# In each step of an attention kernel, TensorE issues the piece of the maxima ahead of the high products instead of between the high and the low products

## The reference

```python
# layer 0, attention over the 4096 positions of a batch, on gn(x)
f = Wq @ xf + bq;  g = Wk @ xf + bk      # 32 channels each
h = Wv @ xf + bv                          # 256 channels
s = einsum('bki,bkj->bij', f, g)          # 4096 x 4096
beta = softmax(s, axis=1)                 # over i
x = x + gamma * einsum('bci,bij->bcj', h, beta)
# layer 1, on gn(x)
y = bn_relu(w1 @ x + b1)                  # 32 channels
packed = all 528 products y[r] * y[c]
x = x + bn_relu(w2 @ packed + b2)
```

## Time and profile before

| | |
|---|---|
| median of three runs | 2136.95 us (2135.04 to 2138.11) |
| the profiled execution's own time | 2135.18 us |
| its span, first to last instruction | 2133.4 us |
| TensorE, matmuls busy | 2081.3 us, 98% |
| DVE busy | 1623.2 us, 76% |
| ScalarE busy | 1608.0 us, 75% |
| GpSimd (POOL) busy | 1321.3 us, 62% |
| mean granted TensorE clock | 0.999 of full |

### The profile page before, as it was taken

How to read it: one execution, slowest core, us unless ns; L and a number is a source line. 1 busy time by engine, 2 the same in 40 slices (tenths; PEclk the granted TensorE clock), 3 DMA queues, 4 the chain that set the end, 5 groups by cost and what they waited for, 6 DMA issues and landing times.

```text
span 2133.4 us, 48577 instructions
## 1 busy us (share of the span) xinstructions
PE 2081.3 (98%) x17838; PEld 1640.4 (77%) x17838; DVE 1623.2 (76%) x3491; ACT 1608.0 (75%) x2582; POOL 1321.3 (62%) x1984
## 2 busy tenths in 40 slices
PE   4899999999999999999999999999999999999999
PEld 2688888888878877877878777777887778777854
DVE  7687877778877777877778887776876767777767
ACT  4577877777777777878777787777877777777767
POOL 3254455556566676776657677676756656566656
PEclk9999999999999999999999999999999999999999
DMA  6054555455467776667378576776635555464622
GB/s 204 21 81 75 75 88 83 84 84 82 81 119 141 138 135 143 135 118 139 71 149 152 117 142 119 142 143 126 130 59 114 117 103 113 97 122 76 118 66 80
DMA packets 592493, 233.63 MB, mean 110 GB/s; under 512 B 541024, under 2 KB 547936, under 8 KB 592224
## 3 DMA queue, kind: packets, MB, share of 16 engines
q1 hardware_dynamic: 592256, 230.53, 56.4%
HBM read 71.83 MB, written 19.92 MB: 43 GB/s over the span
## 4 chain that ended last, share of the span: by engine, by line
PE 92%; DVE 2%; ACT 2%; issue 1%; DMA 1%; SPq 1%; POOL 0%; DVEq 0%; ACTq 0%
PE acc L1763 21%; PE acc L1751 20%; PE acc L1752 20%; PE sps L1576 5%; PE tps L1556 5%; PE acc L1556 5%; PE tps L1627 4%; PE acc L1550 3%; PE tps L1629 2%; PE acc L1627 1%; PE tps L1591 1%; PE tps L1537 1%; PE tps L1613 1%; PE acc L1629 1%; ACT xh L1276 1%
## 5 line engine op out<-in xcount | busy, mean ns | idle before, releaser
L1136 POOL TENSOR_TENSOR kb<-ks,kb 128x512 f16<-128x512 f32 x504 | 599.3, 1194 | 409.6 <-DVE kb L860 235.9
L1314 ACT ACTIVATE ph<-sps,esc 128x512 f16<-128x512 f32 x520 | 356.7, 686 | 345.8 <-PE sps L1576 336.4
L1751 PE MATMUL acc<-hth,ph 128*128 128x257 f16 x2080 | 484.5, 273 | 0.0
L1752 PE MATMUL acc<-htl,ph 128*128 128x256 f16 x2080 | 484.1, 273 | 0.0
L1751 PE MATMUL acc<-hth,kt 128*128 128x257 f16 x2016 | 469.9, 273 | 0.0
L1752 PE MATMUL acc<-htl,kt 128*128 128x256 f16 x2016 | 469.4, 273 | 0.0
L1326 ACT ACTIVATE ks<-ks,kbias,esc 128x512 f32<-128x512 f32 x504 | 407.0, 808 | 0.0
L865 DVE TENSOR_TENSOR pl<-sps,ph 128x512 f16<-128x512 f32 x520 | 355.2, 683 | 48.2 <-ACT sps L1315 46.7
L1315 ACT ACTIVATE sps<-sps,esc 128x512 f32<-128x512 f32 x520 | 340.5, 655 | 0.0
L1763 PE MATMUL acc<-hth,pl 128*128 128x257 f16 x2080 | 318.3, 274 | 0.0
L1763 PE MATMUL acc<-hth,kt 128*128 128x257 f16 x2016 | 308.8, 274 | 0.0
(11 more groups left out here) (253 smaller groups left out, 3606.3 us busy)
## 6 DMA issues: line engine op xcount, KB each, us to landing
rt<-turned SPq DMA_DIRECT2D x96, 256.0 KB, 5.0
xt<-x SPq DMA_DIRECT2D x36, 512.0 KB, 4.3
xb<-x SPq DMA_DIRECT2D x32, 512.0 KB, 5.5
out<-zt SPq DMA_DIRECT2D x45, 256.0 KB, 2.8
kt<-kb SPq DMA_TRANSPOSE x504, 3.2
yb<-turned SPq DMA_DIRECT2D x36, 128.0 KB, 2.8
rt<-turned SPq DMA_DIRECT2D x72, 64.0 KB, 2.3
turned<-yb SPq DMA_DIRECT2D x12, 256.0 KB, 2.1
```

Of the source, the lines that this page charges most:

```text
L1136: tt(kb[:, m % KB_RING, 1], ks[:, m % KS_RING], kb[:, m % KB_RING, 0], ALU.subtract).then_inc(kl_ok, 1)
L1314: A(ph[:, v % SLOTS], sps[v % 2][:], ACT.Exp, scale=esc[:]).then_inc(ph_ok, 1)
L1751: mm(bank[:, 0:C + 1], high[:, q], hth[:, c * QT + q], start=(s8 == 0 and q == 0), stop=False)
L1752: mm(bank[:, 0:C], high[:, q], htl[:, c * QT + q], start=False, stop=False)
```

## The change

The call of `step_piece(u)` moves from behind the eight high products to in front of them, and also in front of the wait for `ph_ok` or for the DMA. Only the first step of each batch keeps the old place, and one wait of the second step of the first batch moves along with the call.

```diff
@@ -1734,6 +1734,10 @@
                                 pe.wait_ge(set_dve, mark["part1"])
                             transposed(G - 1, (t - 4) // 3, 1)
+                        if (b, J, t) == (0, 0, 1):
+                            pe.wait_ge(h_lo, 2 * NCH)
+                        if J or t:
+                            step_piece(u)
                         if kept(u):
@@ -1752,9 +1756,8 @@
                         if (J, t) == (0, 0) and b:
                             pe.wait_ge(h_lo, 2 * (G + NCH))
-                        if (b, J, t) == (0, 0, 1):
-                            pe.wait_ge(h_lo, 2 * NCH)
-                        step_piece(u)
+                        if J == 0 and t == 0:
+                            step_piece(u)
                         if u == 0:
                             scores(SCORED[u])
```

## The result

| | before | changed |
|---|---|---|
| median of 8 runs each | 2135.62 us (2131.79 to 2138.11) | 2142.82 us (2138.84 to 2145.13) |
| ratio | | 1.0033, interval 1.0024 to 1.0042 |
| the profiled execution: its time, its span | 2135.18, 2133.4 us | 2145.13, 2143.3 us |

The change costs 7.2 us, 5.1 to 9.0 by the interval: clearly more than the 0.2% at which a change shows, and less than the 11.2 us forecast.

The account below looks back on a forecast made before the run. TensorE's own instruction stream was taken to bound the kernel. 2135.2 + 0 + 0 + 11.2 = 2146.4 us, forecast as 2148 us because the profiled execution stands 1.8 us below the median; range 2139 to 2160 us.

Parts of the forecast that it names:

- TensorE's stream is the time: TensorE is busy 2081.3 of 2133.4 us, so a change of order can gain only a few microseconds of waits.
- The matmuls' own cost: On TensorE, the piece and the matmuls around it cost the same in the new order: 0 us.
- weight loads as a rival: The piece's weight load shows behind a 56 ns score matmul in 483 steps: up to 20.3 us more, chance 0.08.
- High products issued later: On TensorE, high products come 0.22 us later, with nothing to gain or lose: 0 us.
- DVE's earlier pieces: DVE gets pieces earlier and its 380.9 us of idle time ahead of them largely moves elsewhere: 0 us.
- The bank term: Pieces wait for DVE, in backlogs, to read the bank needed 0.87 us earlier: 11.2 us over 19 places.
- Heads that did move: A backlog's head on DVE: fixed if it had waited for ScalarE, starting earlier if it had waited for its piece.
- my rival, backlogs that feed on themselves: Held TensorE delays scores, ScalarE and then DVE, so later pieces wait too: up to 27 us, chance 0.07.

Follow-up runs that it names:

- e0: The changed kernel run again, unaltered; 2140.16 us, 1.0024 of the kernel before.
- e1: Against the kernel before, the piece is issued after four of the eight high products; 2137.05 us, ratio 1.0010.
- e3: The changed kernel, but in 70 steps around 13 DVE backlogs the piece keeps its old place; 2132.47 us, 0.9992 of the kernel before.
- e4: The kernel before, but with the piece ahead of the high products only in 70 steps around 13 DVE backlogs; 2141.31 us, ratio 1.0037.
- e6: The changed kernel with DVE's normed chunks of step 15 moved to 17 and GpSimd's low part to 18, batch 0, groups 3 to 6; 2139.92 us.

## Why the prediction was right, and where its sizes were off

- **TensorE's stream is the time; the change gains at most microseconds.** Right: the length less holds is 1959.4 to 1960.8 us in before, e0, e1, e3, e4, e6 and the changed kernel. The changed order takes 1.4 us less of it. Some 0.5 us of these are scores that no longer wait for ScalarE's L1307 (1.0 us before, 0.5 now), nearly all of it at one place, told below; for the rest I have no cause.
- **The matmuls' own cost, 0 us, and weight loads as a rival of 20.3 us.** Right, the rival is dead: 56 ns at full clock.
- **High products issued later, 0 us.** Right: no wait of a high product is in the list.
- **DVE's earlier pieces, 0 us.** Right in the price; the size of the move was overestimated. I had expected its idle time ahead of pieces to halve, and it fell by a third.
- **The bank term, 11.2 us.** The mechanism was right (e3, e4, e1, and e6 at step 17), its size too high: 9.0 us of new holds, 8.3 in e0. With the 1.4 us that the rest of the steps got shorter this is the 7.7 us of the steps, where the forecast of 2148 us stood on 11.2. Place by place, forecast against measured, by holds:

| place | forecast | measured |
|---|---|---|
| (0, 0, 16) and 17 | 0.87 | 0.87 |
| (0, 1, 24) | 0.87 | 0.88 |
| (0, 2, 12) and 13 | 0.65 | 1.02 |
| (0, 3, 16) and 17 | 0.69 | 0.42 |
| groups 4 to 6 of batch 0 | 1.08 | 1.09 |
| (0, 7, ...) | 0.62 + 0.49 | 1.29, at step 18 |
| (1, 0, 14) | 0.23 | 0 |
| (1, 1, 5) and 6 | 0.86 | 0.87 |
| (1, 7, 24), (2, 7, 24) | 0.86 | 0.87 |
| (2, 1, 6) to 10 | 0.61 | 1.63 |
| (3, 1, 6) to 10 | 1.67 | 0.31 |
| group 2 of batches 0 to 2, steps 29 | 0.86 + 0.84 | -0.21 |

Five of the twelve lines came out to 0.01 us, by a subtraction from two rows for each place. Of the others some were 3.8 us too high together and some 1.6 us too low, so that the sum is better than its parts: that is luck. In the changed kernel the piece of the earlier trace rows looks like this; the bracket is the wait:

```profile
116.30 0.67 DVE L818 TENSOR_REDUCE mx<-acc 128x1 f32<-128x512 f32 x1
...
117.03 0.39 PE L1556 MATMUL acc<-fst,gst 96*128 96x512 f16 x1 [0.41 <-DVE mx L818]
```

The others failed for reasons that the rows before could only half show:

*Heads that did move (1.9 and 0.3 us too much).* At (0, 2, 29) I took DVE's low part as fixed, since it had waited for ScalarE. But ScalarE had waited for DVE (L638), which got its pieces early. In the changed kernel:

```profile
242.96 0.14 DVE L638 SCALAR_TENSOR_TENSOR nbias<-gsb,rstd 128x2 f32<-128x2 f32 x1
...
243.13 1.52 ACT L1276 ACTIVATE xh<-xb,nbias,rstd 128x512 f16<-128x512 f32 x2
```

The same two in the kernel before, where L638 took 0.81 us and L1276 waited 1.51 us for it:

```profile
239.39 0.81 DVE L638 SCALAR_TENSOR_TENSOR nbias<-gsb,rstd 128x2 f32<-128x2 f32 x1
...
240.24 1.52 ACT L1276 ACTIVATE xh<-xb,nbias,rstd 128x512 f16<-128x512 f32 x2 [1.51 <-DVE nbias L638]
```

One more step back along the waits would have shown that this head was not fixed. In group 2 of batches 1 and 2 it moved by 0.4 us, just what those two places were short of. In group 3 of batch 0 the head moved too, by 0.27 us: ScalarE's work did not hang on scores alone, as I had written, but on a DMA ahead of L1324, for which it waited 1.12 us before and 0.85 us now, and the holds there are 0.42 instead of 0.69 us.

*A backlog that had not been there (1.3 us too little).* The two holds forecast for group 7 of batch 0, 0.62 and 0.49 us at steps 21 and 24, did not come; another of 1.29 us did, at a place whose margin had been 1.44 us. That the line nearly fits is luck. At (0, 7, 18) the two L799 took 2.69 us while GpSimd was at work. DVE and GpSimd in the changed kernel:

```profile
508.12 2.69 DVE L799 TENSOR_SCALAR xn<-xb,rstd,nbias 128x512 f32<-128x512 f32 x2
...
510.74 0.68 DVE L818 TENSOR_REDUCE mx<-tps 128x1 f32<-128x512 f32 x1
```
```profile
508.08 2.45 POOL L1136 TENSOR_TENSOR kb<-ks,kb 128x512 f16<-128x512 f32 x2
```

At the same place before they took 0.99 us, while GpSimd was still at the tile's maximum:

```profile
502.52 0.99 DVE L799 TENSOR_SCALAR xn<-xb,rstd,nbias 128x512 f32<-128x512 f32 x2
```

Against TensorE's low products of step 16 the L799 begin where they began before, but GpSimd's L1136 comes 1.0 us earlier, so that it lies over them. The Trainium skill (SBUF — State Buffer, "SBUF: two separate sides") says that DVE and GpSimd share one pair of ports, and that while the one has it the other fully blocks. The durations here agree with that in kind: two L799 of 1.40 and 1.37 us beside L1136, 0.54 us each without it. That this contention is the cause of this hold is argued from the rows; no run here tested it alone.

*A head that was late for GpSimd (1.0 us too little).* At (2, 1, 6) TensorE was held 0.86 us; then DVE waited for ScalarE, and the piece at (2, 1, 8) was held once more, 0.97 us:

```profile
1139.59 0.63 ACT L1358 ACTIVATE qh<-rt 128x512 f16<-128x512 f32 x1 [1.81 <-POOL rt L1157]
...
1141.51 0.69 DVE L865 TENSOR_TENSOR pl<-sps,ph 128x512 f16<-128x512 f32 x1 [1.21 <-ACT sps L1315]
...
1143.10 0.68 DVE L818 TENSOR_REDUCE mx<-tps 128x1 f32<-128x512 f32 x1
...
1143.83 0.39 PE L1556 MATMUL tps<-fst,gst 96*128 96x512 f16 x1 [0.81 <-DVE mx L818]
```

This looks like my rival, backlogs that feed on themselves, but it is not: ScalarE was late because it had waited 1.81 us for GpSimd's L1157, and that had begun at 1137.84, before TensorE was held at 1139.10. It began 0.95 us later than before, measured from the low products of step 5; why is open. In batch 3 the kernel before already had such a wait of ScalarE (1.80 us at 1644.82) and its hold of 0.90 us, and there the changed kernel paid almost nothing more, 0.31 us where I had forecast 1.67. So these rows hold no case of that rival. Why the first hold in batch 3, at (3, 1, 6), was 0.23 and not 0.80 us stays open; in e0 there was none.

*A hold that took over a wait.* At (0, 2, 12) and 13 the holds are 1.02 us where 0.65 was forecast. But between these two pieces the kernel before had a wait that the changed one no longer has:

```profile
218.45 0.38 PE L1576 MATMUL sps<-gst,fst 128*128 128x128 f16 x4 [0.45 <-ACT gst L1307]
```

Held ahead of this place, TensorE came to it later and found L1307 done. The place costs 1.02 - 0.45 = 0.57 us.

## What to carry to other kernels

Moving a transfer or a matmul to an earlier place in an in-order engine's list also moves the moment at which its buffer must be free. Before doing it, take the start of every instance and the end of the read that it waits for, and subtract: the few instances with less room than the shift are the price, while the many with plenty of room gain nothing if the engine is already the bound. And an instruction put ahead of others shares its wait with all of them, so it belongs where its wait is over.

## What the runs showed of the hardware

The first 80 us, the same in all kernels, took between 78.1 and 83.2 us until the steps began, and the start went with the mean granted clock from 45 to 80 us: it was 1.00 in the three executions whose steps began by 78.94 us, 0.95 in the six from 78.99 to 80.95 us, and 0.90 to 0.85 in the three from 81.33 us on. From 80 to 2060 us it was 1.00 in all twelve. These 5.1 us compare with 6.3 us between the fastest and the slowest of eight runs of the changed kernel, and they are more than several of the effects measured here, so a single execution's total says little at this size while the steps alone repeated within 0.8 us the one time that a kernel was profiled twice. One L799 of DVE took from 532 to 1433 ns in the kernel before, with the same shape each time.
